# Two edge counts in one 16-bit word: a graph network kernel counts pairs of source tiles in one column and reads the bytes as 8-bit float codes

## The chip, the cores and the metric

The kernel runs on one core of one Trainium2 chip. The metric is the device time of one execution in microseconds. The names of the engines are PE (TensorE matmul), PEld (TensorE weight load), DVE (VectorE), ACT (ScalarE), POOL (GpSimd) and SP (SyncE, which here only issues DMA transfers).

## The reference, cut to what matters

The reference is a graph network on 12,500 nodes with 64 features and 200,000 edges (src to dst, sorted by dst). A first block computes one message per edge from the features of its two ends and eight edge attributes, and sums the messages at dst. Then three graph convolutions, three layers of neighbourhood averaging and a last block of two dense layers follow. All of these seven need the same thing, a sum over the edges that end in a node:

```
agg = jax.ops.segment_sum(h[src], dst, num_segments=n)
```

where only `h`, its scaling by the nodes' degrees and the dense weights behind it differ from layer to layer. The edges are the same in every layer, so the sum can be written as a product with a matrix of counts: `counts[source, target]` is the number of edges from the one to the other.

## The kernel before, in words

The program has four parts: `prepare`, `edges`, `after_edges` and `dense`.

`prepare` loads x, computes the normed features and two node tables, and makes for every edge two small numbers. The nodes are cut into 98 source tiles of 128 nodes (`TILES`) and into 196 units of 64 target nodes (`UC`, `UNITS`). A unit's targets are taken in 13 blocks (`UB`) of five targets (`BD`). For an edge of a block, `lane` is the source's place in its tile and `cell` is 5 x (source tile) + (target's place in the block). `ends`, `part`, `near` and `far` are the integer and float arrays in which VectorE builds the two numbers (L360 to L370), TensorE transposes them (L426) and ScalarE writes them out as 16-bit floats (L280).

`edges` runs over 196 groups of 1,024 edges, two in each turn of a loop (q = 0 and 1), and does two jobs side by side. The first is the messages: SP loads the edge attributes (`basis`), the targets (`dst_all`) and a window of node rows, POOL gathers the source rows, TensorE joins both into `ps_u` (`join`, L754 and L756, in halves h = 0 and 1), VectorE multiplies by the attributes into `z` (L651), TensorE multiplies z by the weights into `ps_m` (L773, 64 weight loads and matmuls in eight lots), VectorE adds a bias (L676), ScalarE takes the tanh (L599), and TensorE sums the messages at their targets (`sum_group`, L743), which VectorE adds to `aggT` (L660).

The second job is the counting. For each of the 13 blocks of a unit, VectorE makes `cell_hot`, a row per edge with a one in column `cell` (L643, a ring of seven buffers), and for all 13 blocks at once `lane_hot`, with a one in column `lane` (L636). A matmul of the two (`count`, L734) gives the counts of 128 lanes by 98 x 5 = 490 cells in a bank of PSUM (`ps_c`, two banks in turn). ScalarE copies the bank as 8-bit floats into its place in `unit` (L593), and SP writes a finished unit to the array `counts` in memory (L513). A count of the next block but one waits until its bank is empty (semaphore `emptied`).

The orders are written out by hand. On TensorE a group is: join h = 0, count 0, join h = 1, counts 1 and 2, eight lots of `ps_m` matmuls with counts 3 to 9 between them, count 10, the sum of the group before, counts 11 and 12. On VectorE it is: `to_node` (L630), cells 0 to 10, z for h = 0, bias, z for h = 1, `from_node` (L624), cells 11 and 12, the next group's lanes (L636), `add` (L660).

`dense` runs the seven layers. In each, TensorE multiplies the tables of node features (16-bit floats in two parts) by the counts: 98 source tiles x 28 matmuls of 448 columns (L1199), accumulated over the source tiles in four banks `ps_a`. SP streams the counts through a ring of three slots in chunks of 33, 33 and 32 source tiles (`PARTS`). ScalarE copies a finished bank to `agg` (L1023), and the other matmuls of the layer (L1242 to L1247) work on that.

## Time and profile before

| | |
|---|---|
| time of an execution, median of 3 | 9491.55 us (9488.19 to 9496.71) |
| span of the profiled execution, first to last instruction | 8056.5 us |
| what the median has over that span | 1435.1 us |
| busy in the span: PE, PEld | 7250.3 us, 4945.0 us |
| busy in the span: DVE, ACT, POOL | 3022.3 us, 2022.9 us, 1563.6 us |
| mean granted clock of TensorE | 0.965 |
| DMA | 1927.15 MB, 239 GB/s |

The profile is of one execution; it gives its span and not the whole time. The median of the unprofiled runs is 1435.1 us longer than the span, and that part has no rows. The program falls into three stretches: up to 290 us `prepare` and the start of `edges`, then `edges` to 3983 us, and from 4080 us on `dense`. A busy time is the sum of the instructions' durations with overlaps merged.

### The profile page before, as it was taken

How to read it: one execution, taken by the hardware profiler on the slowest of the kernel's cores; microseconds unless marked ns; L12 is line 12 of the kernel's file. 1: busy time of each engine (PE TensorE's matmuls, PEld its weight loads, DVE VectorE, ACT ScalarE, POOL GpSimd, SP SyncE). 2: the span in 40 equal slices, each digit the busy share in tenths (PEclk: the TensorE clock that was granted, in tenths of full speed). 3: DMA queues.
4: the chain of work that ended last, by engine and by line, in shares of the span. 5: the costliest groups of instructions: out<-in, count | busy, mean ns of one | idle time of the engine just before them, and what ended most of it. 6: DMA issues, size and time to landing. Idle time of an engine off the chain costs nothing. (4 is left out here: it accounts for less than half of the span.)

```text
span 8056.5 us, 132776 instructions
## 1 busy us (share of the span) xinstructions
PE 7250.3 (90%) x44520; PEld 4945.0 (61%) x44520; DVE 3022.3 (38%) x4630; ACT 2022.9 (25%) x3278; POOL 1563.6 (19%) x1655
## 2 busy tenths in 40 slices
PE   4688888888888888888779999999999999999999
PEld 2577777777777777777645555555555555555554
DVE  5566666666666666666540000011100000011000
ACT  3344444444444444444300000000000000000000
POOL 2334433443443344334200000000000000000000
PEclk9799999999999999999889999999999999999999
DMA  3688888888888888888758787877788888888776
GB/s 103 164 213 213 217 210 214 214 217 211 214 216 213 213 214 217 211 214 214 174 200 281 268 281 268 280 269 279 272 295 289 295 289 290 293 290 293 266 267 228
DMA packets 828957, 1927.15 MB, mean 239 GB/s; under 512 B 66366, under 2 KB 123134, under 8 KB 828862
## 3 DMA queue, kind: packets, MB, share of 16 engines
q1 hardware_dynamic: 775564, 1816.94, 74.5%
q0 software_dynamic: 52352, 108.63, 4.3%
q8 instruction: 66, 1.08, 0.1%
q10 hardware_dynamic: 946, 0.26, 0.0%
q14 instruction: 29, 0.24, 0.0%
HBM read 1752.16 MB, written 173.46 MB: 239 GB/s over the span
## 5 line engine op out<-in xcount | busy, mean ns | idle before, releaser
L1199 PE MATMUL ps_a<-ring,table 128*128 128x448 fp8e4 x19208 | 3656.3, 353 | 42.8 <-DVE table L105 42.8
L1199 PEld LDWEIGHTS ps_a<-ring,table 128*128 128x128 f16 x19208 | 1881.8, 98 | 1793.4 <-DVE table L105 44.4
L593 ACT CAST unit<-ps_c 128x490 fp8e4<-128x490 f32 (+1 forms) x2548 | 1641.0, 662 | 1994.7 <-PE ps_c L734 1976.0
L560 POOL DMA_INDIRECT gathered<-u_source,plan x1576 | 1486.8, 943 | 2326.9 <-PE ps_u L756 1773.9
L734 PE MATMUL ps_c<-cell_hot,lane_hot 128*128 128x490 f16 x2548 | 889.2, 370 | 490.5 <-DVE cell_hot L643 490.5
L643 DVE TENSOR_SCALAR cell_hot<-iota_n,cell 128x490 f16<-128x490 f16 x2548 | 728.3, 343 | 378.4 <-PE ps_c L734 378.3
L1023 ACT COPY agg<-ps_a 128x448 f32<-128x448 f32 x196 | 104.3, 532 | 2930.3 <-PE ps_a L1199 2930.3
L773 PEld LDWEIGHTS ps_m<-M_sb,z 128*128 128x128 f32 x6272 | 810.2, 192 | 34.5 <-issue 0.3
L773 PEld LDWEIGHTS ps_m<-M_sb,x_sb 128*128 128x128 f32 x6272 | 810.0, 192 | 13.1
L997 POOL COPY hst<-h 128x896 f32 x28 | 26.4, 943 | 3925.8 <-PE ps_t L1211 2463.0
L773 PE MATMUL ps_m<-M_sb,x_sb 128*128 128x64 f32 x6272 | 784.7, 268 | 0.0
L773 PE MATMUL ps_m<-M_sb,z 128*128 128x64 f32 x6272 | 784.7, 268 | 0.0
L734 PEld LDWEIGHTS ps_c<-cell_hot,lane_hot 128*128 128x128 f16 x2548 | 332.8, 131 | 582.3 <-issue 579.9
L756 PEld LDWEIGHTS ps_u<-ident,gathered 128*128 128x128 f32 x3152 | 485.0, 220 | 245.3 <-issue 245.3
L754 PE MATMUL ps_u<-from_node,window 128*128 128x512 f32 x788 | 521.8, 749 | 107.5 <-issue 71.2
L1144 DVE TENSOR_TENSOR hb<-ps_t,inv 128x448 f32<-128x448 f32 x42 | 26.2, 624 | 1449.1 <-PE ps_t L1245 1449.1
L756 PE MATMUL ps_u<-ident,gathered 128*128 128x128 f32 x3152 | 471.7, 299 | 0.0
L1126 DVE SCALAR_TENSOR_TENSOR hb<-ps_t,inv 128x448 f32<-128x448 f32 x28 | 17.5, 624 | 1029.4 <-PE ps_t L1243 1029.4
L743 PE MATMUL ps_w<-to_node,msg 128*65 128x128 f32 x3152 | 377.9, 273 | 1.7 <-DVE aggT L660 1.7
L636 DVE TENSOR_TENSOR lane_hot<-ps_iota,lane 128x1664 f16<-128x1664 f32 x197 | 370.7, 1882 | 0.0
L743 PEld LDWEIGHTS ps_w<-to_node,msg 128*65 128x65 f32 x3152 | 356.9, 138 | 15.5 <-issue 2.0
L651 DVE TENSOR_TENSOR z<-ps_u,basis 128x2048 f32<-128x2048 f32 x99 | 226.8, 2291 | 241.3 <-PE ps_m L773 241.3
(185 smaller groups left out, 3302.1 us busy)
## 6 DMA issues: line engine op xcount, KB each, us to landing
ring<-counts SPq DMA_DIRECT2D x392, 1848.0 KB, 7.1
ring<-counts SPq DMA_DIRECT2D x196, 1792.0 KB, 7.0
basis<-in_basisT SPq DMA_DIRECT2D x198, 1024.0 KB
x_sb<-in_basisT SPq DMA_DIRECT2D x198, 1024.0 KB
counts<-unit SPq DMA_DIRECT2D x196, 784.0 KB
dst_all<-in_dst_seq SPq DMA_DIRECT2D x198, 512.0 KB
gathered<-u_source,plan POOLq DMA_INDIRECT x1576
window<-u_target SPq DMA_DIRECT2D x198, 64.0 KB
```

What stands on the lines that cost most here:

```text
L560: pool.indirect_dma_start(gathered[q][:, i, :], None, Us, bass.IndirectOffsetOnAxis(ap=T["plan"][:, at:at + 1], axis=0)).then_inc(S[f"rows ...
L593: nc.scalar.copy(unit[q][:, :, BD * i:BD * i + n], got[:, :, 0:n], saturate=False).then_inc(S["emptied"], 1)
L636: nc.vector.tensor_tensor(lane_hot[q][:, :, :], ps_iota[:, :].unsqueeze(1).to_broadcast([P, UB, P]), lanes, ALU.is_equal).then_inc(S["lane ...
L643: nc.vector.tensor_scalar(cell_hot[i % RING][:, :], T["iota_n"][:, :], T["cell"][:, bass.ds(g * UB + i, 1)], None, ALU.is_equal).then_inc( ...
L651: nc.vector.tensor_tensor(z[h][:, :, :], ps_u[h][:, :].unsqueeze(1).to_broadcast([P, 4, 512]), basis[q][:, :, 512 * h:512 * h + 512], ALU. ...
L734: mm(ps_c[(UB * q + i) % 2][:, 0:TILES * BD], lane_hot[q][:, i, :], cell_hot[i % RING][:, :], start=True, stop=True).then_inc(S["counted"], 1)
L743: last = mm(ps_w[0:D + 1, :], msg[q][:, i, :], to_node[q][:, i, :], start=(i == 0), stop=(i == ET - 1))
L754: mm(ps_u[h][:, :], window[q][:, :], from_node[q][:, 512 * h:512 * h + 512], start=True, stop=False)
L756: last = mm(ps_u[h][:, i * P:(i + 1) * P], gathered[q][:, 4 * h + i, :], T["ident"][:, :], start=False, stop=(i == 3))
L773: last = mm(ps_m[q][:, 4 * h + i, :], z[h][:, k, i * P:(i + 1) * P], T["M"][:, k, :], start=(k == 0), stop=(k == 3))
L1023: nc.scalar.copy(agg[:, BC * b:BC * b + BC], ps_a[:, b, 0:BC]).then_inc(S["agg_out"], 1)
L1199: last = mm(ps_a[:, b, 0:BC].rearrange("p (u c) -> p u c", u=BU), table[n % 2][:, k, :], cells, start=(k == 0), stop=(k == TILES - 1))
```

## The change

Two source tiles now share a column. Their 98 tiles make 49 pairs (`PAIRS`), and `cell` is 5 x (pair) + (target's place), so a block has 245 cells (`CELLS`). An edge whose source lies in the odd tile of the pair counts 256 (`ODD`) in place of 1; the new array `worth` holds 1 or 256 for each edge, and VectorE multiplies it in where it makes `cell_hot`. A count in PSUM is then (count of the even tile) + 256 x (count of the odd tile). Two blocks write side by side into one bank, and ScalarE copies the bank once, as 16-bit integers, so that a pair of blocks (a couple, `UP` = 7 of them) is evicted by one instruction and the last block by one of its own.

In memory the word's low byte is the even tile's count and its high byte the odd tile's. `dense` reads the bytes as codes of an 8-bit float: a small count n, read so, has the value n x 2^-9 (`CODE`), and ScalarE multiplies by 512 where it takes `ps_a` out. The matmuls read every second byte. The bytes in all are as many as before; the chunks are now 34, 32 and 32 source tiles.

```diff
-PARTS = [(0, 33), (33, 66), (66, 98)]
+PARTS = [(0, 34), (34, 66), (66, 98)]
...
+CELLS = PAIRS * BD
+ODD = 256.0
+CODE = 2.0 ** -9
...
-            nc.vector.tensor_scalar(part[:, :, :], ends[:, :, :, 0], 7, None, ALU.logical_shift_right)
+            nc.vector.tensor_scalar(part[:, :, :], ends[:, :, :, 0], 8, None, ALU.logical_shift_right)
...
+            ch(nc.vector.tensor_scalar(part[:, :, :], ends[:, :, :, 0], P, None, ALU.bitwise_and))
+            nc.vector.scalar_tensor_tensor(out=far[:, :, :], in0=part[:, :, :], scalar=ODD / P, in1=far[:, :, :], op0=ALU.mult, op1=ALU.add).then_inc(S["cell"], 1)
...
+            dve.wait_ge(S["turned_ev"], BQ // 4)
+            ch(nc.vector.tensor_scalar(T["worth"][:, :], T["cell"][:, :], ODD - 0.5, ODD, ALU.is_gt, ALU.mult))
+            ch(nc.vector.tensor_tensor(T["cell"][:, :], T["cell"][:, :], T["worth"][:, :], ALU.subtract))
+            ch(nc.vector.tensor_scalar(T["worth"][:, :], T["worth"][:, :], 1.0 - 1.0 / ODD, 1.0, ALU.mult, ALU.add))
...
-        cell_hot = [sb(f"cell_hot{i}", [P, TILES * BD], F16) for i in range(RING)]
-        unit = two(sb, "unit", [P, TILES, UC], F8)
+        cell_hot = [sb(f"cell_hot{i}", [P, CELLS], F16) for i in range(RING)]
+        unit = two(sb, "unit", [P, PAIRS, UC], U16)
...
-        taken_out = lambda g, i: 2 + UB * g + (i + 1)
+        taken_out = lambda g, i: 2 + UP * g + (i // 2 + 1)
...
-                        got = ps_c[(UB * q + i) % 2][:, 0:TILES * BD].rearrange("p (k j) -> p k j", j=BD)
-                        nc.scalar.copy(unit[q][:, :, BD * i:BD * i + n], got[:, :, 0:n], saturate=False).then_inc(S["emptied"], 1)
+                        bank = ps_c[(UP * q + c) % 2]
+                        at = 2 * BD * c
+                        if i % 2:
+                            got = bank[:, 0:2 * CELLS].rearrange("p (h k j) -> p k h j", h=2, j=BD)
+                            nc.scalar.copy(unit[q][:, :, at:at + 2 * BD].rearrange("p k (h j) -> p k h j", h=2), got).then_inc(S["emptied"], 1)
+                        else:
+                            got = bank[:, 0:CELLS].rearrange("p (k j) -> p k j", j=BD)
+                            nc.scalar.copy(unit[q][:, :, at:UC], got[:, :, 0:UC - at]).then_inc(S["emptied"], 1)
...
-                        nc.vector.tensor_scalar(cell_hot[i % RING][:, :], T["iota_n"][:, :], T["cell"][:, bass.ds(g * UB + i, 1)], None, ALU.is_equal).then_inc(S["cells"], 1)
+                        nc.vector.tensor_scalar(cell_hot[i % RING][:, :], T["iota_n"][:, :], T["cell"][:, bass.ds(g * UB + i, 1)], T["worth"][:, bass.ds(g * UB + i, 1)], ALU.is_equal, ALU.mult).then_inc(S["cells"], 1)
...
-                        pe.wait_ge(S["emptied"], taken_out(g, i) - 2)
+                        if i % 2 == 0:
+                            pe.wait_ge(S["emptied"], taken_out(g, i) - 2)
                         pe.sem_inc(S["passed"], 1)
-                        mm(ps_c[(UB * q + i) % 2][:, 0:TILES * BD], lane_hot[q][:, i, :], cell_hot[i % RING][:, :], start=True, stop=True).then_inc(S["counted"], 1)
+                        mm(ps_c[(UP * q + i // 2) % 2][:, CELLS * (i % 2):CELLS * (i % 2 + 1)], lane_hot[q][:, i, :], cell_hot[i % RING][:, :], start=True, stop=True).then_inc(S["counted"], 1)
...
-                    nc.scalar.copy(agg[:, BC * b:BC * b + BC], ps_a[:, b, 0:BC]).then_inc(S["agg_out"], 1)
+                    nc.scalar.mul(agg[:, BC * b:BC * b + BC], ps_a[:, b, 0:BC], 1.0 / CODE).then_inc(S["agg_out"], 1)
...
-                        cells = ring[:, s, :, k - k0, :].bitcast(F8)
+                        cells = ring[:, s, :, (k - k0) // 2, :].bitcast(F8).rearrange("p u (c h) -> p u c h", h=2)[:, :, :, k % 2]
```

On TensorE, in the group loop from the second half of the join to the first lots of `ps_m`, the rows before are (L754 and L756 are the join, L734 the counts, L773 the message matmuls):

```order
L754 MATMUL ps_u<-from_node,window 128x512 [waits e_z_done]
L756 MATMUL ps_u<-ident,gathered 128x128 x4
L731 REGISTER_ALU
L734 MATMUL ps_c<-cell_hot,lane_hot 128x490 [waits e_cells,e_emptied]
L731 REGISTER_ALU
L734 MATMUL ps_c<-cell_hot,lane_hot 128x490 [waits e_cells,e_emptied]
L773 MATMUL ps_m<-M_sb,z 128x64 [waits e_m_bias0,e_z_done]
L773 MATMUL ps_m<-M_sb,z 128x64 x3
L731 REGISTER_ALU
L734 MATMUL ps_c<-cell_hot,lane_hot 128x490 [waits e_cells,e_emptied]
```

and at the same place in the changed program (L774 and L776 are the join, L754 the counts, L793 the message matmuls):

```order
L774 MATMUL ps_u<-from_node,window 128x512 [waits e_z_done]
L776 MATMUL ps_u<-ident,gathered 128x128 x4
L750 REGISTER_ALU
L754 MATMUL ps_c<-cell_hot,lane_hot 128x245 [waits e_cells]
L750 REGISTER_ALU
L752 REGISTER_ALU [waits e_cells]
L754 MATMUL ps_c<-cell_hot,lane_hot 128x245 [waits e_emptied]
L793 MATMUL ps_m<-M_sb,z 128x64 [waits e_m_bias0,e_z_done]
L793 MATMUL ps_m<-M_sb,z 128x64 x3
L750 REGISTER_ALU
L754 MATMUL ps_c<-cell_hot,lane_hot 128x245 [waits e_cells]
```

The order is the same; a count has 245 columns in place of 490, and only every second one waits for an empty bank.

On VectorE, at the end of `prepare`, the changed program has these rows from the making of `cell` on (L371 to L379 build `far` and `near`, L381 to L383 work on the transposed array):

```order
L371 SCALAR_TENSOR_TENSOR far<-work,far 128x2560 [waits p_dve]
L372 TENSOR_SCALAR work<-rec 128x2560 [waits p_dve]
L373 SCALAR_TENSOR_TENSOR far<-work,far 128x2560 [waits p_dve]
L375 TENSOR_SCALAR found<-near 128x20 [waits p_cell]
L376 TENSOR_SCALAR work<-rec 128x2560 [waits p_dve]
L377 CAST near<-work 128x2560 [waits p_dve]
L378 TENSOR_REDUCE faults<-found 128x1
L379 TENSOR_REDUCE faults<-faults 128x1 [waits p_dve]
L381 TENSOR_SCALAR worth<-cell 128x2560 [waits p_turned_ev]
L382 TENSOR_TENSOR cell<-cell,worth 128x2560 [waits p_dve]
L383 TENSOR_SCALAR worth<-worth 128x2560 [waits p_dve]
L385 TENSOR_SCALAR fault_row<-psB 1x1 [waits p_faultsum,p_dve]
```

Five of them are new: L372, L373 and L381 to L383. The first two stand ahead of the signal `cell` for which TensorE's transposes wait.

## Rows read from the trace of the kernel before

**Rows 1.** Busy time, granted clock and DMA share by stretch (windows)

```profile
core 0: us, PE busy (x) PEld busy (x) DVE busy (x) ACT busy (x) POOL busy (x), PEclk, DMA share, GB/s
1400.00:2400.00 1000.00, 847.75 (x6015) 721.31 (x6014) 667.74 (x1066) 473.22 (x746) 401.90 (x426) 0.96 0.82 213
...
5300.00:6000.00 700.00, 700.00 (x3924) 391.23 (x3922) 100.68 (x119) 32.18 (x67) 4.67 (x5) 1.00 0.80 278
```

**Rows 2.** Page, costliest groups: count, mean ns, idle before and its releaser

```profile
L1199 PE MATMUL ps_a<-ring,table 128*128 128x448 fp8e4 x19208 | 3656.3, 353 | 42.8 <-DVE table L105 42.8
...
L593 ACT CAST unit<-ps_c 128x490 fp8e4<-128x490 f32 (+1 forms) x2548 | 1641.0, 662 | 1994.7 <-PE ps_c L734 1976.0
...
L734 PE MATMUL ps_c<-cell_hot,lane_hot 128*128 128x490 f16 x2548 | 889.2, 370 | 490.5 <-DVE cell_hot L643 490.5
```

**Rows 3.** Line L734 by itself: durations in ns, first and last start

```profile
L734 PE MATMUL ps_c<-cell_hot,lane_hot x2548: 367/370/615, 292.6 to 3981.9; 128*128 128x490 f16 x196
```

**Rows 4.** Timeline of VectorE over one group: start, us, line, count, wait

```profile
2001.53 0.69 DVE L676 TENSOR_TENSOR msg<-ps_m,iib 128x512 f32<-128x512 f32 x1 [1.89 <-PE ps_m L773]
...
2004.34 0.74 DVE L624 TENSOR_SCALAR from_node<-dst_all,nodeid 128x1024 f32<-128x1024 int32 x1
2005.00 0.60 DVE L643 TENSOR_SCALAR cell_hot<-iota_n,cell 128x490 f16<-128x490 f16 x2
...
2008.64 2.14 DVE L643 TENSOR_SCALAR cell_hot<-iota_n,cell 128x490 f16<-128x490 f16 x8
...
2019.95 0.69 DVE L676 TENSOR_TENSOR msg<-ps_m,iib 128x512 f32<-128x512 f32 x1 [1.89 <-PE ps_m L773]
...
2039.07 0.69 DVE L676 TENSOR_TENSOR msg<-ps_m,iib 128x512 f32<-128x512 f32 x1 [1.89 <-PE ps_m L773]
```

**Rows 5.** Timeline of PE over the same group and the next one

```profile
2005.49 0.63 PE L734 MATMUL ps_c<-cell_hot,lane_hot 128*128 128x490 f16 x2 [2.04 <-DVE cell_hot L643]
...
2009.12 0.37 PE L734 MATMUL ps_c<-cell_hot,lane_hot 128*128 128x490 f16 x1 [0.83 <-DVE cell_hot L643]
...
2012.44 0.37 PE L734 MATMUL ps_c<-cell_hot,lane_hot 128*128 128x490 f16 x1
2012.65 1.00 PE L773 MATMUL ps_m<-M_sb,z 128*128 128x64 f32 x8
2013.49 0.37 PE L734 MATMUL ps_c<-cell_hot,lane_hot 128*128 128x490 f16 x1
...
2019.75 0.37 PE L734 MATMUL ps_c<-cell_hot,lane_hot 128*128 128x490 f16 x1
...
2023.91 0.62 PE L734 MATMUL ps_c<-cell_hot,lane_hot 128*128 128x490 f16 x2 [2.04 <-DVE cell_hot L643]
2025.07 2.05 PE L754 MATMUL ps_u<-from_node,window 128*128 128x512 f32 x2 [0.54 <-issue]
```

**Rows 6.** Busy time and granted clock in a stretch of the second group (windows)

```profile
2025.00:2028.40 3.40, 3.33 (x11) 2.31 (x12) 3.40 (x9) 0.36 (x1) 0.00 (x0) 0.55 1.00 226
```

**Rows 7.** Timeline of VectorE at the end of `prepare`

```profile
228.96 1.49 DVE L362 TENSOR_SCALAR far<-near 128x2560 f32<-128x2560 f32 x1
...
233.35 2.83 DVE L364 SCALAR_TENSOR_TENSOR far<-work,far 128x2560 f32<-128x2560 int32 x1
236.21 0.18 DVE L366 TENSOR_SCALAR found<-near 128x20 f32<-128x20 f32 x1
...
247.13 0.15 DVE L372 TENSOR_SCALAR fault_row<-psB 1x1 int32<-1x1 f32 x1 [7.42 <-PE psB L430]
```

**Rows 8.** Timeline at the end of `prepare`: transposes, and the last copy of `cell`

```profile
239.70 3.50 PE L426 MATMUL psA<-ident,far 128*128 128x128 f32 x16 [1.50 <-ACT ud L274]
...
243.72 0.59 ACT L280 CAST cell<-psB 128x512 f16<-128x512 f32 x1
```

**Rows 9.** Timeline of ACT in `dense`: the copies of finished banks

```profile
5303.27 0.53 ACT L1023 COPY agg<-ps_a 128x448 f32<-128x448 f32 x1 [36.55 <-PE ps_a L1199]
5309.33 0.53 ACT L1023 COPY agg<-ps_a 128x448 f32<-128x448 f32 x1 [5.52 <-PE ps_a L1199]
```

More of the change, by code:

```diff
@@ L8 @@
 F8 = mybir.dt.float8e4
+U16 = mybir.dt.uint16
 I32 = mybir.dt.int32
@@ L34 @@
 A_BYTES = UNITS * P * TILES * UC
-PARTS = [(0, 33), (33, 66), (66, 98)]
+PAIRS = TILES // 2
+PARTS = [(0, 34), (34, 66), (66, 98)]
 CHUNKS = len(PARTS) * BANKS
@@ L42 @@
 UB = -(-UC // BD)
+UP = -(-UB // 2)
+CELLS = PAIRS * BD
+ODD = 256.0
+CODE = 2.0 ** -9
 BLOCKS = UNITS * UB
@@ L109, in build @@
     x = w["x"]
-    A = nc.dram_tensor("counts", (A_BYTES,), U8, kind="Internal").ap()
+    A = nc.dram_tensor("counts", (A_BYTES // 2,), U16, kind="Internal").ap()
     Us = nc.dram_tensor("u_source", (NP, 2 * D), F32, kind="Internal").ap()
@@ L138, in build @@
             T["lane"] = esb("lane", [P, BQ * P + UB], F16)
-            T["iota_n"] = esb("iota_n", [P, TILES * BD], F16)
+            T["iota_n"] = esb("iota_n", [P, CELLS], F16)
+            T["worth"] = esb("worth", [P, BQ * P], F16)
             prepare(nc, T, x, w, Us, Ud, irregular)
@@ L166, in prepare @@
         iota_i = sb("iota_i", [P, W + 1 + BQ], I32)
-        iota_c = sb("iota_c", [P, TILES * BD], I32)
+        iota_c = sb("iota_c", [P, CELLS], I32)
         iota_p = sb("iota_p", [P, 1], F32)
@@ L363, in _ @@
             ch(nc.vector.tensor_tensor(far[:, :, :], far[:, :, :], near[:, :, :], ALU.add))
-            nc.vector.scalar_tensor_tensor(out=far[:, :, :], in0=part[:, :, :], scalar=float(BD), in1=far[:, :, :], op0=ALU.mult, op1=ALU.add).then_inc(S["cell"], 1)
+            ch(nc.vector.scalar_tensor_tensor(out=far[:, :, :], in0=part[:, :, :], scalar=float(BD), in1=far[:, :, :], op0=ALU.mult, op1=ALU.add))
+            ch(nc.vector.tensor_scalar(part[:, :, :], ends[:, :, :, 0], P, None, ALU.bitwise_and))
+            nc.vector.scalar_tensor_tensor(out=far[:, :, :], in0=part[:, :, :], scalar=ODD / P, in1=far[:, :, :], op0=ALU.mult, op1=ALU.add).then_inc(S["cell"], 1)
             dve.wait_ge(S["cell"], 1)
@@ L891, in dense @@
         table = [sb(f"table{i}", [P, TILES, 2 * D], F16) for i in range(2)]
-        ring = sb("ring", [P, SLOTS, BU, PARTS[0][1], UC], U8)
+        ring = sb("ring", [P, SLOTS, BU, PARTS[0][1] // 2, UC], U16)
         agg = sb("agg", [P, GC], F32)
@@ L913, in dense @@
         rows = sb("rows_d", [P, XT, D], F32)
-        ring_bytes = ring[:, :, :, :, :].rearrange("p s u k c -> p (s u k c)")
-        hot = [ring_bytes[:, 2 * GC * i:2 * GC * (i + 1)].bitcast(F16) for i in range(XT)]
+        ring_words = ring[:, :, :, :, :].rearrange("p s u k c -> p (s u k c)")
+        hot = [ring_words[:, GC * i:GC * (i + 1)].bitcast(F16) for i in range(XT)]
         V = {n: sem("g_" + n) for n in "table ends rows known gathered placed hot used".split()}
@@ L1086, in place_edges @@
                     for i in range(XT):
-                        nc.vector.tensor_scalar(hot[i], places[:, :], place[:, i:i + 1], None, ALU.is_equal).then_inc(V["hot"], 1)
+                        nc.vector.tensor_scalar(hot[i], places[:, :], place[:, i:i + 1], CODE, ALU.is_equal, ALU.mult).then_inc(V["hot"], 1)
             def loop(start, body):
```

22 lines of the change are left out of this document (11 added, 11 removed).

## The prediction

> **What bounds the kernel now.** I read the busy times by stretch first [rows 1]. In `dense` TensorE is busy for all of 700 us at full clock; its pace there is that of the L1199 matmuls. Two copies of finished banks stand 6.06 us apart [rows 9], and 32 source tiles lie between them (the last chunk), so one matmul takes 6.06 / 32 = 0.189 us, and 19,208 of them [rows 2] make 3,637 us. Nothing there waits for ScalarE, and TensorE's own wait in that line is 42.8 us in all [rows 2].
>
> In `edges` no engine is full: PE is busy 848 of 1,000 us, DVE 668, ACT 473, with DMA at 0.82 [rows 1]. So a loop of waits must bound it. The first L734 is at 292.6 us and the last at 3981.9 [rows 3]; the last is count 12 of the 196th group, some 15 us behind its count 0 (2009.12 to 2023.91 and a bit, [rows 5]), so a group takes (3689.3 - 15) / 195 = 18.84 us. The timelines show the loop. VectorE waits for the last `ps_m` matmuls before the bias at 2001.53 [rows 4]; then, without a pause, come bias, z, `from_node`, cells 11 and 12, lanes, `add`, `to_node` and cell 0 of the next group at 2008.64 [rows 4]. TensorE waits for that cell and starts count 0 at 2009.12 [rows 5]: 7.59 us behind the bias. From there TensorE runs through to count 10 at 2019.75 [rows 5], 10.63 us, and the bias follows 0.20 us later at 2019.95 [rows 4]. 7.59 + 10.63 + 0.20 = 18.42 us, which is the distance of the two biases.
>
> The next group takes 19.12 us (2019.95 to 2039.07, [rows 4]). The wait for cell 11 is the same 2.04 us there, another 0.54 us of issue follows at the turn of the loop [rows 5], and then the granted clock is 0.55 over 3.4 us [rows 6], so nearly all of it is at the lower level (1.2 GHz, not 2.4). The join takes 2.05 us for its first two matmuls and comes later than the cell. So of the mean of 18.84 us, 18.42 are the loop's and 0.42 the clock's.
>
> **The change part by part.**
>
> *Counts on TensorE.* From one count to the next lie 1.05 us (2012.44 to 2013.49); count to following matmul is 0.21 us (to 2012.65), so the eight `ps_m` matmuls take 0.84, 0.105 each [rows 5]. 490 columns at 2.4 GHz are 0.204 us, so the count's 0.21 is its columns. With 245 it would be 0.102 us, but the matmul behind it needs its weights loaded meanwhile, and where matmul follows matmul here that sets 0.105 us. So a count falls from 0.204 to about 0.107, a gain of 0.097 us. Ten counts (0 to 9) lie on the 10.63 us stretch: -0.97 us a group. Counts 10 to 12 lie ahead of TensorE's wait for the cell and give nothing.
>
> *Cells on VectorE.* Three of them (11, 12 and 0) lie on the 7.59 us stretch. The eight in a row take 2.14 us [rows 4], a pace of 0.257 us after the first's 0.34. What would 245 elements with a second scalar take? The fixed part is about 0.16 us: 2,560 elements in 1.49 us and 20 in 0.18 [rows 7] give 0.516 ns an element. L624, with one scalar read from memory, takes 0.74 us for 1,024 elements [rows 4], 0.21 over its elements, so that scalar costs about 0.05. L643's 490 elements in 0.34 us are then 0.13 us of stream. Halved, they save 0.065 us, and the second scalar (`worth`) takes back perhaps 0.05, perhaps nothing. I take 0. The bounds: -0.06 us a cell if the second scalar is free; and if the new form ran at the 1.04 ns an element of L364 (2.83 us less 0.18 for 2,560, [rows 7]), 0.255 + 0.26 = 0.52 us, +0.18 a cell. Three of them: -0.18 to +0.54 us a group.
>
> The Trainium skill ("VectorE: DVE Perf Modes", section "Mode 2×_2P — use both read ports for one tensor") asks for the outermost dimension to be even, or odd and the same in source and destination. 245 is odd and the same on both sides, so by it the fast mode stays, and an odd row alone would not cost the 0.52 us; no row here has an odd length in this form.
>
> *Copies on ScalarE.* 13 of 0.66 us become 7 of about as many elements, so 8.6 us a group become about 4.6. ScalarE waited for the counts for 1,976 us in all and TensorE never for it [rows 2]: worth nothing. Its cover is wide: a bank is needed again two couples later, about 1.9 us, and even a copy of 1.0 us (source in runs of five, 2-byte output) stays under that.
>
> *Clock.* The wait of 2.04 us for cell 11 grows to about 2.14, since TensorE is earlier by a count and VectorE is not. So the clock goes on falling, but the turns now last another time and a fall will meet another part of the group. Bounds: no loss, or a loss of 0.84 us, twice the present 0.42 (a fall in every group). I choose 0.25 us, a bit over half: a pair of groups becomes shorter against the same waits, and where the lower clock meets the stretch in which the join has 0.83 us of slack ahead of count 0 [rows 5] it costs less.
>
> *Loads.* DMA works 0.82 of 18.84 us, 15.4 us a group [rows 1], at unchanged bytes. At 17.7 us that is 0.87. No wait for it shows in the loop; it would bind below about 16.
>
> *`prepare`.* L372 and L373 are as L362 and L364, 1.49 and 2.83 us [rows 7], 4.3 in all, ahead of the signal that came at 236.2. TensorE only began its transposes at 239.70, held by ScalarE [rows 8], so 3.5 of the 4.3 are hidden: +0.85 us. The last copy of `cell` then ends at 243.72 + 0.59 + 0.85 = 245.2 [rows 8]; three operations on 2,560 16-bit elements follow. By L643's stream (0.27 ns an element) two take 0.85 us, the third has two tensors and lies between 0.85 and 2.8, I take 1.5: VectorE is ready at 248.4, against 247.13 for L372 before [rows 7]. +1.3 us, once.
>
> *`dense`.* Same matmuls, columns and bytes; a chunk of 34 for one of 33. The moving operand is now read a byte in every two. L734 reads 16-bit elements, so two bytes a column, at one column a cycle [rows 5]; the strided bytes come from no more memory than that. I take 0. ScalarE's multiplication in place of a copy is hidden behind 5.52 us of waiting [rows 9], but for the last group of all (0.1 us).
>
> **The sum.** Per group 0.97 + (0.42 - 0.25) = 1.14 us, times 196 = 223 us; less 1.3 is 222. The span goes from 8056.5 to about 7834.5 us. What the median has over the span (1435.1 us) has no rows, and nothing in the change bears on a launch, so I carry it over: 9491.55 - 222 = 9270 us.
>
> **Rivals.**
>
> *The strided bytes are slower (slower than before).* No row reads every second byte. If a matmul of L1199 grew by more than 222 / 19,208 = 11.6 ns on 189, the gain is gone; TensorE has no slack to hide it [rows 1]. At 1.2 columns a nanosecond in place of 2.4 it would be +0.187 x 19,208 = 3,590 us, 12,860 in all; at a tenth more +360, 9,630. Against it stands L734's pace. 9 in 100.
>
> The Trainium skill ("SBUF — State Buffer", section "Door 1: The DMA port swizzle (why `[64,N]` ≈ `[32,N]`)", the note on "cachelines") says that reads which touch the same 16-byte line at least twice run at full bandwidth. With a step of two bytes a line is touched eight times, so by it this rival would not come; no run shows it yet.
>
> *The cells become dearer, or the clock takes the gain.* At +0.18 a cell: 1.14 - 0.54 = 0.60, 118 us, 9,375 us. With the clock's loss doubled in its place: 0.97 - 0.42 = 0.55, 108 us, 9,385. For it speaks that the wait ahead of the fall is there in every group already. 10 in 100.
>
> *More than forecast.* The clock stays up and the second scalar is free: 0.97 + 0.42 + 0.18 = 1.57 us, 308 us, 9,185 us. 8 in 100.
>
> *The loop is held by something else, so that the shorter counts give nothing.* It could be the loads, if 0.82 is as much as they can take: 9,490. Against it: DMA has a share of 1.00 in the 3.4 us of [rows 6], so 0.82 is a mean with idle time in it. 3 in 100.
>
> **How the numbers follow.** The forecast holds 70 in 100. Its range is 9,190 (the clock stays up and half of the cells' best case) to 9,350 (the clock costs what it does now and the cells 0.1 us more each, 0.97 - 0.3 = 0.67 us, 131 us, 9,360, cut a little); with parts of the neighbours it holds 8 in 10. A measurement of this kernel tells about 0.2% (19 us) from no change. Faster 0.88: all cases but the strided one and the held loop; within it 0.03; slower 0.09.
>
> **What would show it.** L754 (counts) at a pace of 0.107 us ahead of the next matmul; count 0 to count 10 in 9.7 us, and 17.4 us from bias to bias at full clock; a mean group of 17.7 us. Cells at a pace of 0.25 us. ScalarE's copies seven a group, near 0.66 us. In `dense` still 6.06 us between banks: the first place to look, since anything else there outweighs all the rest. `fault_row` some 1.3 us later. The prediction is wrong if that pace grows, if `from_node` begins to wait for its load, or if the clock falls in every group.

## The result and the profile after

The changed kernel takes 8874.58 us (median of 4, 8867.31 to 8882.06), the kernel before in the same job 9493.82 (9488.19 to 9496.71): a ratio of 0.9347, 95% interval [0.9333, 0.936]. It is 619 us faster. The forecast was 222, with 9190 to 9350 us as its range; the sign was right and the gain was 2.8 times the forecast one. Three executions of the later jobs took 12,826 to 27,849 us at a granted clock of 0.52 to 0.62, and the ratios leave them out.

The page of the changed kernel, its span and its costliest groups, in the columns of [rows 2]:

```profile
span 8872.1 us, 130626 instructions
...
L1219 PE MATMUL ps_a<-ring,table 128*128 128x448 fp8e4 x19208 | 3654.7, 353 | 45.7 <-DVE table L111 45.7
...
L754 PE MATMUL ps_c<-cell_hot,lane_hot 128*128 128x245 f16 x2548 | 697.0, 290 | 510.4 <-DVE cell_hot L662 204.0
...
L609 ACT CAST unit<-ps_c 128x490 uint16<-128x490 f32 x1176 | 651.4, 570 | 3613.9 <-PE ps_c L754 2536.1
```

The span is 2.5 us below the median. Before, span and median stood 1435 us apart, and the prediction took that for a constant outside the span. Now it is gone. The last row has a second sign: ScalarE was idle for 3613.9 us ahead of its copies, and only 2536.1 of them are put down to the count (before, 1976.0 of 1994.7, [rows 2]).

The windows that answer to [rows 1]:

```profile
1400.00:2400.00 1000.00, 795.08 (x4870) 673.91 (x4870) 534.27 (x860) 179.58 (x345) 326.84 (x347) 0.78 0.67 174
...
6000.00:7000.00 1000.00, 1000.00 (x5564) 553.45 (x5562) 117.56 (x140) 42.49 (x87) 6.55 (x7) 1.00 0.81 281
```

`dense` is as before: TensorE busy throughout at full clock. In `edges` the changed kernel looks *worse* than the profile of before: a clock of 0.78 for 0.96, and 4,870 matmuls in 1,000 us for 6,015. The line of the counts, beside [rows 3]:

```profile
L754 PE MATMUL ps_c<-cell_hot,lane_hot x2548: 265/268/413, 303.8 to 4796.6; 128*128 128x245 f16 x196
```

(4796.6 - 303.8 - 15) / 195 = 22.96 us a group, where 17.7 was forecast and the profile of before had 18.84. By the two profiles the change made `edges` 800 us slower, while by the clock of the runs the kernel became 619 us faster. So the profiled execution of before can't have been like the timed ones; experiment 1 tests that.

The timeline of all engines around 2,000 us shows where the time of a group goes now (start, duration, then what it waited for):

```profile
2000.13 0.94 POOL L573 DMA_INDIRECT gathered<-u_source,plan  x1 [13.77 <-PE ps_u L776]
...
2000.75 0.27 PE L754 MATMUL ps_c<-cell_hot,lane_hot 128*128 128x245 f16 x1
...
2001.14 0.57 ACT L609 CAST unit<-ps_c 128x490 uint16<-128x490 f32 x1 [0.48 <-PE ps_c L754]
...
2002.64 0.27 PE L754 MATMUL ps_c<-cell_hot,lane_hot 128*128 128x245 f16 x1
...
2002.75 1.01 PE L793 MATMUL ps_m<-M_sb,z 128*128 128x64 f32 x8
...
2003.59 0.27 PE L754 MATMUL ps_c<-cell_hot,lane_hot 128*128 128x245 f16 x1
...
2004.54 0.27 PE L754 MATMUL ps_c<-cell_hot,lane_hot 128*128 128x245 f16 x1
...
2005.98 0.57 ACT L609 CAST unit<-ps_c 128x490 uint16<-128x490 f32 x1 [4.27 <-PE ps_c L754]
...
2006.69 0.27 PE L754 MATMUL ps_c<-cell_hot,lane_hot 128*128 128x245 f16 x1 [1.03 <-ACT unit L609]
...
2008.72 0.37 PE L754 MATMUL ps_c<-cell_hot,lane_hot 128*128 128x245 f16 x1 [0.92 <-issue]
...
2008.89 0.94 POOL L573 DMA_INDIRECT gathered<-u_source,plan  x1 [0.30 <-issue]
...
2010.86 1.42 PE L793 MATMUL ps_m<-M_sb,x_sb 128*128 128x64 f32 x6 [1.14 <-issue]
...
2010.88 2.29 DVE L670 TENSOR_TENSOR z<-ps_u,basis 128x2048 f32<-128x2048 f32 x1 [9.35 <-remote]
2011.77 1.04 ACT L609 CAST unit<-ps_c 128x490 uint16<-128x490 f32 x2 [5.22 <-remote]
...
2012.48 0.36 PE L754 MATMUL ps_c<-cell_hot,lane_hot 128*128 128x245 f16 x1 [0.20 <-ACT unit L609]
```

The z at 2010.88 needs TensorE's fourth lot of `ps_m` (2002.75), which stands ahead of the count at 2003.59. Experiment 8 has the same pair undisturbed, and there z starts 0.20 us behind that count; here 7.29. The copy of the couple whose second count began at 2002.64 should start at about 2003.03 (0.39 us behind it, as 2001.14 follows a count at 2000.75); it starts at 2005.98, and the next, due at 2004.93, at 2011.77. Were the consumers late themselves? The trace also keeps the time of each semaphore's update, which no view prints. A count's update is recorded 0.28 us behind its start where nothing is disturbed (2001.03 for 2000.75). For the count of 2002.64 it is recorded at 2005.86, for that of 2003.59 at 2010.89, and the fourth lot's at 2010.86. VectorE and ScalarE start 0.02 and 0.12 us behind theirs, so it is TensorE's signals that come late.

Whether only the signal is late or also the work behind it, the trace doesn't tell, as the ends of matmuls in it are modelled. For the work speaks that TensorE comes out of a gap of its own at 2010.86, 0.02 us ahead of the z; the same is so, within 0.06 us, for 53 of the 81 waits of z of more than 3 us from 1,000 to 3,000 us (for none of 73 in the kernel before as profiled in experiment 1). By the starts of its matmuls TensorE runs on for as long as it has an empty bank, waits until 2006.69 for the late copy, and stutters until 2012.48. GpSimd issues its eight gathers from 2000.13 to 2009.83, and the gap begins within them and ends some 2 us behind. The clock follows, in windows of 3 us:

```profile
2003.00:2006.00 3.00, 2.66 (x25) 2.52 (x24) 0.00 (x0) 0.02 (x1) 2.39 (x3) 1.00 1.04 331
2006.00:2009.00 3.00, 1.39 (x11) 1.30 (x12) 0.00 (x0) 0.54 (x1) 2.08 (x4) 0.79 0.79 297
2009.00:2012.00 3.00, 1.61 (x9) 1.64 (x8) 1.12 (x1) 0.23 (x1) 0.83 (x1) 0.50 0.17 44
2012.00:2015.00 3.00, 2.80 (x14) 2.48 (x14) 3.00 (x3) 1.44 (x3) 0.00 (x0) 0.50 0.00 0
```

TensorE idled for half of 2006 to 2012, and from 2009 on it was granted the lower level (1.2 GHz). The waits from 1,000 to 3,000 us name the same place, for the changed kernel and then for the kernel before as profiled (us in total, times, longest):

```profile
DVE z L670 <- remote: 648.7, 73, 10.1
ACT unit L609 <- remote: 464.8, 91, 6.0
```

```profile
DVE z L651 <- PE ps_m L773: 263.5, 107, 2.5
```

"remote" is the profile's word where a signal ended the wait and no instruction ended near enough to it to be its sender. The trace on which the prediction rests has none of it in this stretch.

### The profile page after: what moved, and what is told of

It is laid out like the page before. It is cut to its first block and busy times, and to the rows that moved or that the text cites. A ratio compares the mean times of both kernels' runs of the same rounds, so it can differ in the third digit from the quotient of the medians.

```text
span 8872.1 us, 130626 instructions
## 1 busy us (share of the span) xinstructions
PE 7688.3 (87%) x44520; PEld 5304.7 (60%) x44520; DVE 3011.9 (34%) x4635; ACT 1100.0 (12%) x2102; POOL 1566.4 (18%) x1655
## 5 line engine op out<-in xcount | busy, mean ns | idle before, releaser
L1219 PE MATMUL ps_a<-ring,table 128*128 128x448 fp8e4 x19208 | 3654.7, 353 | 45.7 <-DVE table L111 45.7
L793 PE MATMUL ps_m<-M_sb,x_sb 128*128 128x64 f32 x6272 | 990.5, 297 | 320.4 <-issue 315.6
L793 PEld LDWEIGHTS ps_m<-M_sb,x_sb 128*128 128x128 f32 x6272 | 942.0, 220 | 364.4 <-issue 362.7
L754 PE MATMUL ps_c<-cell_hot,lane_hot 128*128 128x245 f16 x2548 | 697.0, 290 | 510.4 <-DVE cell_hot L662 204.0
L609 ACT CAST unit<-ps_c 128x490 uint16<-128x490 f32 x1176 | 651.4, 570 | 3613.9 <-PE ps_c L754 2536.1
L662 DVE TENSOR_SCALAR cell_hot<-iota_n,cell,worth 128x245 f16<-128x245 f16 x2548 | 721.3, 340 | 351.3 <-PE ps_c L754 327.2
L793 PE MATMUL ps_m<-M_sb,z 128*128 128x64 f32 x6272 | 755.6, 269 | 0.0
L793 PEld LDWEIGHTS ps_m<-M_sb,z 128*128 128x128 f32 x6272 | 748.6, 192 | 1.4
L754 PEld LDWEIGHTS ps_c<-cell_hot,lane_hot 128*128 128x128 f16 x2548 | 320.5, 126 | 663.9 <-issue 656.4
L763 PE MATMUL ps_w<-to_node,msg 128*65 128x128 f32 x3152 | 678.7, 400 | 22.7 <-issue 20.6
L763 PEld LDWEIGHTS ps_w<-to_node,msg 128*65 128x65 f32 x3152 | 609.8, 218 | 61.7 <-issue 61.3
L776 PEld LDWEIGHTS ps_u<-ident,gathered 128*128 128x128 f32 x3152 | 480.3, 218 | 240.9 <-issue 240.9
L774 PE MATMUL ps_u<-from_node,window 128*128 128x512 f32 x788 | 519.0, 746 | 115.0 <-issue 78.7
L670 DVE TENSOR_TENSOR z<-ps_u,x_sb 128x2048 f32<-128x2048 f32 x98 | 224.6, 2291 | 794.3 <-remote 626.5
L776 PE MATMUL ps_u<-ident,gathered 128*128 128x128 f32 x3152 | 473.5, 300 | 0.0
L1043 ACT ACTIVATE agg<-ps_a 128x448 f32<-128x448 f32 x196 | 106.6, 544 | 2910.3 <-PE ps_a L1219 2910.3
```

Of the source, the lines that this page charges most:

```text
L609: nc.scalar.copy(unit[q][:, :, at:at + 2 * BD].rearrange("p k (h j) -> p k h j", h=2), got).then_inc(S["emptied"], 1)
L662: nc.vector.tensor_scalar(cell_hot[i % RING][:, :], T["iota_n"][:, :], T["cell"][:, bass.ds(g * UB + i, 1)], T["worth"][:, bass.ds(g * UB ...
L670: nc.vector.tensor_tensor(z[h][:, :, :], ps_u[h][:, :].unsqueeze(1).to_broadcast([P, 4, 512]), basis[q][:, :, 512 * h:512 * h + 512], ALU. ...
L754: mm(ps_c[(UP * q + i // 2) % 2][:, CELLS * (i % 2):CELLS * (i % 2 + 1)], lane_hot[q][:, i, :], cell_hot[i % RING][:, :], start=True, stop ...
L763: last = mm(ps_w[0:D + 1, :], msg[q][:, i, :], to_node[q][:, i, :], start=(i == 0), stop=(i == ET - 1))
L774: mm(ps_u[h][:, :], window[q][:, :], from_node[q][:, 512 * h:512 * h + 512], start=True, stop=False)
```

## The experiments

Runs of one job share a chip and their runs of the kernel before. The jobs differ, and that is part of the finding, so this is where the kernel before stood, first. The record names six different chips for jobs 2 to 7 and none for job 1 and the profile of before, so what belongs to a job can't be told from what belongs to a chip.

| job | experiments | before, us | changed kernel, us |
|---|---|---|---|
| 1 | the result | 9493.82 | 8874.58 |
| 2 | 1 to 4 | 9337.2 | 8711.74 |
| 3 | 5 to 8 | 9493.8 | |
| 4 | 9 to 12 | 8046.14 | (10 and 12 stand for it: 7892.18, 7880.4) |
| 5 | 13 to 16 | 9353.96 | 8719.54 |
| 6 | 17 | 9491.88 | 8860.32 |
| 7 | 18 | 9356.14 | |

Theory A, called "theory R" (room) in the expectations: TensorE's signals come late in each group, and the changed kernel gains by its room, that is how many blocks TensorE may count ahead of ScalarE's copies: four (two banks of two blocks) where it was two (two banks of one). Theory B, built on the prediction's reading: 1435 us lie outside the span, in the launch, and against the prediction the change touched them. Theory C: fewer copies on ScalarE are what pays. Theory D: the shorter counts pay more than 0.097 us each.

### 1 to 4: the two halves of the change, and a doubled count

*e1_before_again* and *e4_after_again* have no edit. *e2_single_copies* takes the changed kernel back to a bank and a copy for each block, at 245 cells:

```diff
-        taken_out = lambda g, i: 2 + UP * g + (i // 2 + 1)
+        taken_out = lambda g, i: 2 + UB * g + (i + 1)
...
-                        mm(ps_c[(UP * q + i // 2) % 2][:, CELLS * (i % 2):CELLS * (i % 2 + 1)], ...
+                        mm(ps_c[(UB * q + i) % 2][:, 0:CELLS], ...
```

*e3_counts_twice* issues each count's matmul a second time, into the same place, so that the result is the same.

> The kernel before, unchanged. In the changed kernel a group of the edge stage takes about 23.5 us at a granted clock of 0.79, and its span (8872.1 us) is within 3 us of its time, while the profiled execution of before had a span 1435 us shorter than its median. Theory S (stalls): the timed executions of before are not like the profiled one; their span is within some us of 9490, the edge stage takes (9490 - 8056) / 196 = 7.3 us a group more, 26 us, at a clock below 0.85, with TensorE and VectorE held up while no wait of the program is open. Rival (launch): the extra 1435 us lie outside the span in every execution of before, the span is 8056 us again at clock 0.96, and the changed kernel got rid of something outside the span.

> The changed kernel, but every block is copied out of PSUM by an instruction of its own (13 of 245 elements a group in place of 7 of up to 490), each count waits for its own bank again; 245 columns and the 16-bit words stay. If the gain comes from the shorter counts on TensorE: within 0.5% of the changed kernel, 8870 us. If it comes from the fewer copies and signals of ScalarE: it goes back most of the way, above 9200 us.

> The changed kernel, but every count matmul is issued twice into the same place, so that TensorE spends as long on it as before (2 x 245 columns), with the copies in pairs kept. If the gain comes from the shorter counts: back to 9450 to 9500 us. If from the fewer copies: it stays near 8870 us, at most 0.97 x 196 = 190 us more.

> The changed kernel again, as the measure for the others on this chip: 8875 us within 0.3%, dense part as before (6.05 us between two banks). If the time of both kernels hangs on the phase between the loop and the clock's changes, single executions will differ by more than 1%.

Measured, each against 9337.2: e1 9330.18 (0.9991 [0.9982, 1.0001]); e2 9161.13 (0.9804 [0.9787, 0.9822]); e3 9003.69 (0.9639 [0.9618, 0.966]); e4 8711.74 (0.9325 [0.9308, 0.9342]).

The span of the kernel before, profiled anew, and its rows that answer to [rows 3] and [rows 1]:

```profile
span 9345.1 us, 132776 instructions
```

```profile
L734 PE MATMUL ps_c<-cell_hot,lane_hot x2548: 367/370/615, 306.6 to 5270.8; 128*128 128x490 f16 x196
```

```profile
1400.00:2400.00 1000.00, 741.54 (x4385) 633.79 (x4386) 483.62 (x776) 336.60 (x542) 293.12 (x311) 0.81 0.60 156
```

The span is within 15 us of the median, and a group takes (5270.8 - 306.6 - 15) / 195 = 25.38 us for the 18.84 of the trace that was read. Theory B falls: nothing of note lies outside the span (1.7 us of this execution's 9346.79). (25.38 - 18.84) x 196 = 1,282 us, and this job's median lies 9337.2 - 8056.5 = 1,281 us above the profiled execution: the group loop holds all of it.

Narrow counts alone give 176 us (9337.2 to 9161.13), and the pairs on top of them 449. That kills theory D as the main cause. e3 prices a count by itself: 8711.74 to 9003.69 is 292 us for 2,548 more matmuls, 0.115 us each, near the forecast's 0.107. It is more than the 190 us expected as the most, which had priced ten of the thirteen counts of a group.

### 5 and 6: copies or room?

*e5_halves_apart* keeps the banks and the waits and copies the two halves of a couple by two instructions. *e6_one_couple_ahead* keeps the one copy and lets TensorE start a couple only when the one before is taken out:

```diff
-                            nc.scalar.copy(unit[q][:, :, at:at + 2 * BD].rearrange("p k (h j) -> p k h j", h=2), got).then_inc(S["emptied"], 1)
+                            for h in range(2):
+                                got = bank[:, CELLS * h:CELLS * (h + 1)].rearrange("p (k j) -> p k j", j=BD)
+                                last = nc.scalar.copy(unit[q][:, :, at + BD * h:at + BD * (h + 1)], got)
+                            last.then_inc(S["emptied"], 1)
```

```diff
-                            pe.wait_ge(S["emptied"], taken_out(g, i) - 2)
+                            pe.wait_ge(S["emptied"], taken_out(g, i) - 1)
```

> The changed kernel, but ScalarE copies the two halves of a couple's bank by two instructions, both after the couple's second count; TensorE still waits once a couple. So 13 copies again, but two couples of room. Theory R (room): in each group TensorE's signals come late for some 4 us, and what the pairs give is that TensorE may run up to four counts ahead of the copies in place of two; the number of copies is worth nothing. Then within 0.5% of the changed kernel (8712 us on the chip of the second job). Theory C (copies): fewer instructions and signals of ScalarE are the gain; then near e2, 5% above the changed kernel.

> The changed kernel, but a couple's first count waits until the couple just before it is out, not the one before that: copies in pairs and 245 columns stay, the room falls from two couples to one. Theory R: slower than the changed kernel by at least as much as e2, 5% or more (9150 us or above against 8712). Theory C: at most some tens of us slower, the 0.6 us of a copy at the places where it now shows.

Measured against 9493.8: e5 8894.16 (0.9363 [0.9347, 0.9379]), e6 9833.62 (1.0356 [1.0338, 1.0373]). Beside the result (0.9347, in a job whose kernel before took the same 9493.8), thirteen copies in place of seven cost 0.0016 of the time, 15 to 20 us, and the two intervals overlap: theory C falls. Against e2, which has thirteen copies of the same size too (0.9804 of its kernel before), e5 has the room on top. Taking the room away costs 11% and puts the changed kernel behind the one before. The page's row of the counts in e6:

```profile
L754 PE MATMUL ps_c<-cell_hot,lane_hot 128*128 128x245 f16 x2548 | 795.7, 312 | 1333.7 <-ACT unit L609 951.5 <-issue 209.4 <-DVE cell_hot L662 172.5
```

Now TensorE waits 951.5 us for ScalarE's copies, and a group takes 28.00 us. The copies themselves are as short as in the changed kernel:

```profile
L609 ACT CAST unit<-ps_c 128x490 uint16<-128x490 f32 x1176 | 667.6, 568 | 4232.2 <-PE ps_c L754 2816.7
```

568 ns for 570. They are late, not long.

### 7 and 8: what makes the signals late

Both leave work out. *e7_no_target_load* loads 8 columns of `dst_all` a group inside the loop in place of all 1,024. *e8_one_gather* issues one of the eight gathers of source rows in every group but the first two, so the other seven tiles keep old rows:

```diff
-                    for i in range(ET):
+                    for i in range(ET if t == 0 else 1):
```

(and the waits on `rows0` and `rows1` count accordingly).

> The changed kernel, but in the loop the load of dst_all moves 8 columns in place of 1,024 (512 KB a group less; the from_node matrix then mostly holds old targets, the messages are not the reference's). The late signals begin about when these packets are done and the window's, the counts' and the gathers' begin. If the dense burst of this load holds them up: the stall of 4 us a group goes, 700 us or more faster. If it is the mere sum of traffic: a share of it, 100 to 300 us. If it is the gathers or the counts' write: under 50 us.

> The changed kernel, but after the first two groups POOL issues one of a group's eight gathers (the rest of the gathered rows are old, the messages are not the reference's). The stall ends close to the last gather's packets in every second group. If the gathers hold TensorE's signals up: no update later than 1 us, 700 us or more faster (a group near 17.7 us, as first forecast). If not: under 100 us.

Measured: e7 8891.11 (0.937 [0.9354, 0.9385]), no different from e5 in the same job and 17 us above the result; e8 7893.37 (0.8316 [0.8303, 0.833]). The broadcast load is not the cause; without seven gathers the kernel drops by some 980 us (8874.58 of job 1 less 7893.37, with equal kernels before). VectorE's z and bias in e8, and the count ahead of the z:

```profile
2015.76 0.27 PE L754 MATMUL ps_c<-cell_hot,lane_hot 128*128 128x245 f16 x1
...
2015.96 2.29 DVE L670 TENSOR_TENSOR z<-ps_u,basis 128x2048 f32<-128x2048 f32 x1 [2.27 <-PE ps_m L793]
...
2019.76 0.69 DVE L695 TENSOR_TENSOR msg<-ps_m,iib 128x512 f32<-128x512 f32 x1 [1.50 <-PE ps_m L793]
...
2037.41 0.69 DVE L695 TENSOR_TENSOR msg<-ps_m,iib 128x512 f32<-128x512 f32 x1 [1.50 <-PE ps_m L793]
```

The z follows the count by 0.20 us, its wait is 2.27 us with the releaser named (the changed kernel had 9.35 of "remote"), and the next bias comes 17.65 us after the last. In a job whose kernel before takes as long as that of the result, this is the loop that the prediction described.

### 9 to 12: a job without the disturbance

*e9_before_one_gather* is e8's edit on the kernel before. *e10_three_banks* gives the changed kernel a third bank for counts (its place comes from `ps_iota`, which moves to SBUF). *e11_gathers_half_wide* fetches half of each gathered row's bytes, and so leaves wrong features in place; *e12_four_gathers* issues four of eight.

```diff
-        ps_c = two(ps, "ps_c", [P, 512])
+        ps_c = [ps(f"ps_c{i}", [P, 512]) for i in range(3)]
...
-                            pe.wait_ge(S["emptied"], taken_out(g, i) - 2)
+                            pe.wait_ge(S["emptied"], taken_out(g, i) - (2 if UP * q + i // 2 < 2 else 3))
```

> The kernel before with one of a group's eight gathers, as in e8 (old gathered rows, the messages are not the reference's). With it gone the signals come on time, and the comparison with e8 (7893 us) gives the worth of the change in an undisturbed loop. The prediction's sum (0.97 us a group from ten counts, the clock's share on top) says 222 us: about 8115 us, a group of 18.4 us at full clock against 17.4. If the rest of the measured gain (619 us) is the room: no more than that 222 here. If it is something else: e9 is 400 us or more above e8.

> The changed kernel with three banks for the couples (the iota that stood in a bank of PSUM is read from SBUF in its place). Theory R: room for six counts outlasts more of the 4 us of late signals; another 1 us a group or more, 200 us, near 8670 us. Rival: TensorE is then held by something else that needs a signal (the z matmuls wait for VectorE, which waits for TensorE's m_done), and it gains under 50 us; VectorE may lose some by reading both operands from SBUF.

> The changed kernel, but the loop's gathers fetch 256 bytes a row from x in place of 512 from u_source (eight a group, 128 rows each, half the bytes; not the reference's messages). If the bytes of the gathers hold the signals up: half of e8's gain, some 490 us. If the number of gathers and rows does: within 50 us of the changed kernel.

> The changed kernel with four of the eight gathers in the loop at full width (the other rows old). If the number of gathers counts: half of e8's gain or more, 490 us; if only the first or the last of them holds the signals up: near the changed kernel or near e8.

Here the kernel before took 8046.14 us (13 executions, 8038.72 to 8056.71): the time that the profile of the prediction had. e9 8037.14 (0.999 [0.9981, 1.0]), e10 7892.18 (0.9808 [0.9792, 0.9825]), e11 7883.68 (0.98 [0.9784, 0.9817]), e12 7880.4 (0.9792 [0.9776, 0.9809]). In this job the gathers cost nearly nothing (9 us for seven of eight), e10 with its third bank is no faster than e12, and what was meant to tell bytes from count (e11 against e12) tells neither.

What the job does give is the change without the disturbance. The counts of e9 and of e12:

```profile
L734 PE MATMUL ps_c<-cell_hot,lane_hot x2548: 367/370/615, 282.8 to 3964.1; 128*128 128x490 f16 x196
```

```profile
L754 PE MATMUL ps_c<-cell_hot,lane_hot x2548: 265/268/413, 293.7 to 3806.9; 128*128 128x245 f16 x196
```

(3964.1 - 282.8 - 15) / 195 = 18.80 us a group against 17.94: 0.86 us, and 8037.14 - 7880.4 = 157 us in all. (The counts of e12 begin 10.9 us later; e10, with the same `prepare`, begins them at 286.1, so most of that is scatter between executions.) e10 against the kernel before, with all its gathers, gives 154. That is what the forecast of 222 was about. One group of e12, to be read beside [rows 4, 5]:

```profile
2010.65 0.69 DVE L695 TENSOR_TENSOR msg<-ps_m,iib 128x512 f32<-128x512 f32 x1 [1.50 <-PE ps_m L793]
...
2014.61 0.61 PE L754 MATMUL ps_c<-cell_hot,lane_hot 128*128 128x245 f16 x2 [2.14 <-DVE cell_hot L662]
...
2017.76 2.11 DVE L662 TENSOR_SCALAR cell_hot<-iota_n,cell,worth 128x245 f16<-128x245 f16 x8
...
2018.33 0.27 PE L754 MATMUL ps_c<-cell_hot,lane_hot 128*128 128x245 f16 x1 [0.46 <-DVE cell_hot L662]
...
2021.45 0.27 PE L754 MATMUL ps_c<-cell_hot,lane_hot 128*128 128x245 f16 x1
...
2021.56 1.01 PE L793 MATMUL ps_m<-M_sb,z 128*128 128x64 f32 x8
...
2022.40 0.27 PE L754 MATMUL ps_c<-cell_hot,lane_hot 128*128 128x245 f16 x1
...
2028.10 0.27 PE L754 MATMUL ps_c<-cell_hot,lane_hot 128*128 128x245 f16 x1
...
2028.30 0.69 DVE L695 TENSOR_TENSOR msg<-ps_m,iib 128x512 f32<-128x512 f32 x1 [1.50 <-PE ps_m L793]
```

and the windows from bias to bias over this group and the next two:

```profile
2010.65:2028.30 17.65, 14.31 (x115) 12.47 (x114) 12.46 (x21) 4.28 (x8) 3.77 (x4) 1.00 0.81 208
2028.30:2045.94 17.64, 14.29 (x115) 12.46 (x114) 12.46 (x20) 4.28 (x8) 3.79 (x4) 1.00 0.83 216
2045.94:2064.40 18.46, 15.56 (x115) 13.41 (x114) 12.46 (x20) 4.28 (x8) 3.78 (x4) 0.91 0.82 217
```

Bias to count 0 takes 7.68 us, count 0 to count 10 9.77, and the bias follows 0.20 later: 17.65. Here a group with the clock at full speed is followed by one like it, and only then the clock falls.

### 13 to 16: the same edits once more, beside each other

> The changed kernel again. Theory: its gain has two parts, about 160 to 220 us from the shorter counts wherever it runs, and the rest from the room, only where TensorE's signals come late. So if the kernel before takes about 8050 us in this job, the changed one takes 7830 to 7890; if before takes 9340 to 9490, it takes 0.933 to 0.935 of that.

> The changed kernel with one couple of room in place of two, as e6. If before takes about 8050 us in this job: within 50 us of the changed kernel, since a copy of 0.6 us then shows at few places. If before takes 9340 or more: 1.036 of before, as in e6.

> The changed kernel with one of eight gathers in the loop, as e8. If before takes about 8050 us in this job: within 0.3% of the changed kernel. If before takes 9340 or more: 7893 us, as in e8.

> Three banks for the couples, as e10. If before takes about 8050 us in this job: 7890 us, no better than two banks. If before takes 9340 or more: by theory R 200 us or more below the changed kernel.

The edits are those of e4 (none), e6, e8 and e10. Measured against 9353.96: e13 8719.54 (0.9321 [0.9298, 0.9345]), e14 9731.25 (1.04 [1.0374, 1.0427]), e15 7898.66 (0.8444 [0.8422, 0.8465]), e16 8738.7 (0.9342 [0.9318, 0.9366]). In one job now: the room is worth 1,012 us, the seven gathers cost 821, and a third bank brings nothing. The wait that room can take away is gone in e16: of 2 ms, TensorE's counts waited 100.1 us for ScalarE's copies in e13 and never in e16. What is left is the z; in e16 the largest wait of VectorE is still

```profile
DVE z L670 <- remote: 570.5, 79, 9.2
```

(513.6 in e13), and TensorE needs that z, however many banks are empty. The gain of room ends there.

### 17 and 18: the result again, and half of the gathers

> The changed kernel once more. If before takes about 8050 us in this job: 7830 to 7890 us, a group of 17.4 us at full clock, the counts' part of the prediction (e15 without gathers took 7899, so 7830 would need the clock to stay up as well). If before takes 9340 or more: 0.932 to 0.935 of it.

> The changed kernel with four of the eight gathers in the loop, as e12. If before takes 9340 us or more in this job: halfway between the changed kernel and e8, some 8380 us, if each gather holds TensorE's signals up for its share; near 7900 us if only the gathers that run while TensorE is in the message matmuls do. If before takes about 8050 us: 7880 us again, as e12.

e17 (no edit): 8860.32 against 9491.88, 0.9332 [0.9316, 0.9348]; a fourth job with the same gain. e18 (e12's edit): 8101.6 against 9356.14, 0.8659 [0.8645, 0.8674], 19.04 us a group. Taking the changed kernel of jobs 2 and 5 (8716 us on average; their kernel before is within 20 us of this job's) and e15's 7899, leaving out four gathers gives 8716 - 8102 = 614 us of the 817 that leaving out seven gives. It fits neither of the two expected times (8380 and 7900). So the loss grows with the number of gathers, but not in proportion: the four left out here are 57% of the seven and carry 75%.

## Why the prediction was wrong, and what in it was right

**The loop, right, its gain a little large.** In the undisturbed job the wait for the cell is 2.14 us, as forecast, and a count is followed by its `ps_m` matmul after 0.11 and by the next count after 0.95 (2021.45, 2021.56, 2022.40 in e12), as forecast. Count 0 to 10 took 9.77 for 9.7: the seven counts in a row gave 0.66 us together and the first three 0.20, 0.86 where 0.97 was forecast. And bias to count 0, which the prediction left alone, grew from 7.59 to 7.68. So a group at full clock is 17.65 us where 17.45 was worked out, a gain of 0.77 and not 0.97.

**The clock's term, right.** "I choose 0.25 us, a bit over half." e12 has 17.94 - 17.65 = 0.29 us, for 0.42. Per group 0.77 + (0.42 - 0.29) = 0.90; e9 and e12 measure 0.86. This is the 154 to 157 us of job 4: the loop's term was too large by 0.20 us x 196 = 39 us (0.11 of the 0.20 in the counts, 0.09 in the stretch ahead of count 0), and the rest of the distance to 222 is in the clock (0.29 for 0.25), the means of the two kernels (18.80 for 18.84) and the start. The forecast's range means gains of 142 to 302, so it holds this part. (Its lower end comes out at 9,203 us by the terms named for it, 0.97 + 0.42 + 0.09 = 1.48 us a group, and not at 9,190.)

**The failing step.** "What the median has over the span (1435.1 us) has no rows, and nothing in the change bears on a launch, so I carry it over." The 1435 us were inside the program, in executions other than the one profiled: span and median agree within 0.3% in every later run, and where a group of the kernel before was looked at (e1) it took 25.38 us for 18.84, which is all of the difference. The profiled execution of before was like those of job 4. All rows of the prediction describe it, and none shows the late signals, where the change earns most of its time. The priced loop gives 157 us of the gain; the other 460 or so stood in no term of the sum, and that they too were a gain is luck: with half of the room, as in e6, the same narrow counts in couples lose 340 us.

**The term that this hid.** "Copies on ScalarE ... worth nothing ... Its cover is wide." The number of copies is worth nothing, as e5 shows. But the cover of 1.9 us stands against signals that come 3 to 7 us late (2005.98 for 2003.03, 2011.77 for 2004.93). What the pairs change is how far TensorE gets meanwhile. A count and a lot of `ps_m` take 0.95 us, so four blocks of room are some 3.8 us of work and two are 1.9, an estimate from e12's pace. Of the gain of 625 us in job 2, 176 come with narrow counts alone and 449 with the pairs on top, and e6 and e14, which give TensorE half of the room and that by whole couples, lose all of it and more.

**Cells, right.** The page's row of `cell_hot` has a mean of 340 ns, for 343 on the page of before, and eight take 2.11 us for 2.14; a second scalar at half the elements comes out even.

```profile
L662 DVE TENSOR_SCALAR cell_hot<-iota_n,cell,worth 128x245 f16<-128x245 f16 x2548 | 721.3, 340 | 351.3 <-PE ps_c L754 327.2
```

The Trainium skill ("VectorE: DVE Perf Modes", section "Mode 2×_2P — use both read ports for one tensor") lets an odd outermost dimension keep this mode where it is the same in source and destination, as 245 is. The trace agrees: at the 0.52 us of the upper bound the eight would take over 4 us.

**`dense`, right.** The copies of two finished banks stand where the prediction told to look first:

```profile
7005.42 0.54 ACT L1043 ACTIVATE agg<-ps_a 128x448 f32<-128x448 f32 x1 [5.51 <-PE ps_a L1219]
7011.47 0.54 ACT L1043 ACTIVATE agg<-ps_a 128x448 f32<-128x448 f32 x1 [5.51 <-PE ps_a L1219]
```

6.05 us for 6.06, and TensorE's busy time in that line 3654.7 for 3656.3. A moving operand of every second byte costs nothing here, and the rival of the slower strided bytes is dead. That is what the Trainium skill ("SBUF — State Buffer", section "Door 1: The DMA port swizzle (why `[64,N]` ≈ `[32,N]`)", the note on "cachelines") states of reads that touch a 16-byte line at least twice.

**`prepare`, nearly right.** From L371 to `fault_row` lie 15.88 us (243.73 to 259.61), where the same stretch took 13.78 before (233.35 to 247.13, [rows 7]): +2.1 us for +1.3. L371 itself stands 10.4 us later than before it did, ahead of all new rows; e10 in job 4 has the same row at 225.27, so that is scatter between executions.

```profile
243.73 2.82 DVE L371 SCALAR_TENSOR_TENSOR far<-work,far 128x2560 f32<-128x2560 int32 x1
...
257.10 1.49 DVE L382 TENSOR_TENSOR cell<-cell,worth 128x2560 f16<-128x2560 f16 x1
...
259.61 0.15 DVE L385 TENSOR_SCALAR fault_row<-psB 1x1 int32<-1x1 f32 x1 [0.15 <-PE psB L443]
```

**What stays open.** That the late signals need the gathers is shown by leaving seven or four of eight out (e8, e15, e18); by which path the gathers do it is not, nor whether TensorE's work is late with its signals. Whether it is their packets, their bytes or GpSimd's own work was to be told by e11, which fell on a job without the effect. TensorE's own stutter in the same stretch ("issue", 0.92 and 1.14 us) may have the same cause or another. Why jobs 1 to 3 and 5 to 7 show it and job 4 doesn't is not known, and the chip may be what differs; the kernel before settles at three values, 8046, about 9345 and 9493. The gathers ran in job 4 too, so they are not enough by themselves. No kernel that computes everything was shown to be faster than the changed one.

## What to carry to other kernels

Hold the profile's span against the median before reading anything else. If they differ by more than the runs do among themselves, the trace is of another execution than the timed ones; a gap of 15% is no constant to be added, it is the first thing to explain, and a rival of its own.

Judge the room between two engines by the latest signal between them, not by the consumer's mean duration. Here halving the copies was worth nothing and doubling what may stand in a bank was worth 449 us; and room stopped paying where the same engine needed another late signal, as the third bank showed.

## What of the hardware had not been expected

In the group shown, signals from TensorE to VectorE and ScalarE were recorded up to 7.3 us after the start of the matmul that sends them, with GpSimd's indirect DMAs under way (a z 7.29 us behind a count that it follows by 0.20 in e8). Six of the seven jobs show the longer times that go with it. In the two where it was measured, seven of eight gathers a group cost the changed kernel 821 us (e15 beside e13) and some 980 us (e8); in the undisturbed job the same seven cost the kernel before 9 us (e9).
